# Subtracting the softmax's maximum as the bias of eight small exponentials on ScalarE, in place of one VectorE subtraction per half of the heads

## What is computed

```python
x = x + attn(cond1(x), Wq, Wk, Wv, Wo)   # cond1: per sequence a 64x64 matrix and a bias
x = x + ffn(cond2(x), w_up, w_down)      # quantised, with Walsh-Hadamard transforms
# attn, 16 heads of 32:
scores = q @ k.T / sqrt(32) + alibi_causal_bias      # 64 x 64 per sequence and head
attn   = softmax(scores, axis=-1)                    # exp(s - max) / sum
out    = (attn @ v) @ Wo.T
# ffn:
h = hbitlinear(x, w_up)       # fwht, quantise per token by its absolute maximum, matmul
h = square(relu(h))
y = hbitlinear(h, w_down)
```

## Time and profile before

| | before |
|---|---|
| median of 3 runs | 871.18 us (870.59 to 871.32) |
| profiled execution, its own time | 873.74 us |
| its span | 871.9 us |
| busy: PE, DVE, ACT, POOL | 797.4, 661.9, 376.2, 266.9 us |
| mean granted TensorE clock | 0.977 |

### The profile page before, as it was taken

The page is one execution under the profiler, slowest core; times in us unless marked ns, Lnnn a source line. Parts: engine busy times, 40 slices in busy tenths (PEclk is TensorE's granted clock), DMA queues, the critical chain, the costliest instruction groups (busy, mean ns, idle before and its releaser), DMA issues.

```text
span 871.9 us, 19069 instructions
## 1 busy us (share of the span) xinstructions
PE 797.4 (91%) x7625; PEld 681.0 (78%) x7625; DVE 661.9 (76%) x1243; ACT 376.2 (43%) x687; POOL 266.9 (31%) x324
## 2 busy tenths in 40 slices
PE   6965899999999999999999999999999999998777
PEld 4855788888888888888888888888888888786563
DVE  3455777887788778877788788877887788777864
ACT  1564245444433444444434454444334444443321
POOL 1202332333233333333233323332333333322311
PEclk8968999999999999999999999999999999999989
DMA  8521111111111101111111011111111110000000
GB/s 276 171 97 31 29 30 33 41 43 44 44 44 31 39 30 32 43 44 44 43 36 36 30 31 44 43 44 43 44 30 34 34 34 26 28 26 27 13 12 13
DMA packets 38285, 39.65 MB, mean 45 GB/s; under 512 B 21172, under 2 KB 22324, under 8 KB 38196
## 3 DMA queue, kind: packets, MB, share of 16 engines
q1 hardware_dynamic: 34436, 33.48, 12.5%
q10 hardware_dynamic: 3760, 4.95, 1.7%
HBM read 30.02 MB, written 8.39 MB: 44 GB/s over the span
## 4 chain that ended last, share of the span: by engine, by line
PE 59%; DVE 17%; POOL 10%; ACT 7%; issue 6%; ACTq 1%; DMA 1%; POOLq 0%; DVEq 0%
PE bank L322 35%; DVE hid L223 13%; POOL gT L223 9%; PE bank L499 8%; PE bank L442 7%; PE bank L412 4%; PE bank L520 3%; ACT hid L660 2%; ACT hid L658 2%; ACT gT L683 2%; PE bank L430 1%; DMA k_bd<-in_L_attn_Wk_dram 1%; ACTq L598 1%; DVE s L761 0%; DVE srow L765 0%
## 5 line engine op out<-in xcount | busy, mean ns | idle before, releaser
L223 DVE TENSOR_TENSOR hid<-hid 128x256 f32<-128x256 f32 (+1 forms) x192 | 136.1, 748 | 5.6 <-ACT hid L660 0.9
L223 POOL TENSOR_TENSOR hid<-hid 128x256 f32<-128x256 f32 x128 | 100.0, 801 | 118.4 <-DVE hid L860 115.9
L223 POOL TENSOR_TENSOR gT<-gT 128x256 f32<-128x256 f32 x124 | 87.7, 729 | 157.2 <-ACT gT L683 154.8
L499 PE MATMUL bank<-cst_sb,hid 128*128 128x128 f32 x512 | 68.5, 289 | 25.6 <-DVE hid L223 25.6
L499 PEld LDWEIGHTS bank<-cst_sb,hid 128*128 128x128 f32 x512 | 62.2, 198 | 31.8 <-DVE hid L223 31.8
L939 POOL TENSOR_TENSOR s<-s,srow 128x512 f32<-128x512 f32 x32 | 33.5, 1046 | 172.2 <-DVE srow L782 164.5
L322 PE MATMUL bank<-h_hi,wk_hi 128*128 128x256 f32 x256 | 77.4, 303 | 9.0 <-ACT v_bd L566 5.3
L678 ACT ACTIVATE late<-bank,sc 128x1024 f32<-128x1024 f32 x32 | 35.8, 1117 | 98.1 <-DVE sc L895 98.1
L918 POOL TENSOR_TENSOR h_lo<-h_sum,h_hi 128x512 fp32r<-128x512 f32 x32 | 41.0, 1285 | 113.0 <-ACT h_hi L553 105.7
L322 PE MATMUL bank<-h_hi,wq_hi 128*128 128x256 f32 x256 | 75.4, 295 | 0.0
L322 PE MATMUL bank<-h_lo,wk_hi 128*128 128x256 f32 x256 | 73.1, 286 | 0.0
(11 more groups left out here) (114 smaller groups left out, 2004.7 us busy)
## 6 DMA issues: line engine op xcount, KB each, us to landing
x_in<-in_x_dram SPq DMA_DIRECT2D x32, 256.0 KB, 2.8
x_res<-in_x_dram SPq DMA_DIRECT2D x32, 256.0 KB, 2.6
out_dram<-late SPq DMA_DIRECT2D x32, 256.0 KB, 3.1
w_bd<-in_L_cond_weights_dram SPq DMA_DIRECT2D x126, 16.0 KB, 2.0
bias_in<-in_fside_8xS_dram SPq DMA_DIRECT2D x62, 32.0 KB, 2.9
k_bd<-in_L_attn_Wk_dram ACTq DMA_DIRECT2D x1, 1024.0 KB, 5.5
s<-in_L_attn_Wq_dram ACTq DMA_DIRECT2D x1, 1024.0 KB, 8.4
v_bd<-in_L_attn_Wv_dram ACTq DMA_DIRECT2D x1, 1024.0 KB, 10.7
```

What stands on the lines that cost most here:

```text
L223: eng.tensor_tensor(dv[:, :, n], sv[:, :, 0], sv[:, :, 1], op).then_inc(done, 1)
L499: mm = pe.matmul(ps01[:, m * P:(m + 1) * P], hid[:, 1, m, :], had, start=True, stop=True)
```

## The change

The subtraction (part 2) is taken out of `softmax` on DVE, in both halves. `exp` on ACT becomes eight instructions of 128 x 64, one per head, whose bias operand is that head's entry in `srow`. So that the maximum can be used as it stands, DVE writes the negated score (the scale is negative and the ALiBi bias is subtracted), takes the minimum, and the exponential has scale -1: exp(-s' + min s') = exp(s - max s). The counts of `d_soft` fall from 14 to 12 a step. Nothing moves between DMA queues, PE and POOL.

```diff
+            def exp(p, c, half):
+
+                act.wait_ge(d_soft, p * 12 + 2 * half + 2)
+                for h in range(8 * half, 8 * half + 8):
+                    e = act.activation(s[:, c % 2, h, :], s[:, c % 2, h, :], ACT.Exp, bias=srow[:, 0, h:h + 1], scale=-1.0)
+                e.then_inc(a_exp, 1)
...
                 if attn:
-                    act.wait_ge(d_soft, p * 14 + 3)
-                    act.activation(s[:, c % 2, 0:8, :], s[:, c % 2, 0:8, :], ACT.Exp).then_inc(a_exp, 1)
+                    exp(p, c, 0)
...
                 if attn:
-                    act.wait_ge(d_soft, p * 14 + 6)
-                    act.activation(s[:, c % 2, 8:16, :], s[:, c % 2, 8:16, :], ACT.Exp).then_inc(a_exp, 1)
+                    exp(p, c, 1)
...
                     if part == 0:
                         dve.wait_ge(s_s, p * 2 + half + 1)
-                        dve.scalar_tensor_tensor(s[:, c % 2, hs, :].rearrange("p h k -> p (h k)"), bank[half], DH ** -0.5,
-                                                 alibi[:, hs, :].rearrange("p h k -> p (h k)"), ALU.mult, ALU.add).then_inc(d_soft, 1)
-                    elif part == 1:
+                        dve.scalar_tensor_tensor(s[:, c % 2, hs, :].rearrange("p h k -> p (h k)"), bank[half], -DH ** -0.5,
+                                                 alibi[:, hs, :].rearrange("p h k -> p (h k)"), ALU.mult, ALU.subtract).then_inc(d_soft, 1)
+                    else:
                         dve.wait_ge(d_soft, c0 + 1)
-                        dve.tensor_reduce(srow[:, 0, hs], s[:, c % 2, hs, :], AX.X, ALU.max).then_inc(d_soft, 1)
-                    else:
-                        dve.wait_ge(d_soft, c0 + 2)
-                        dve.tensor_tensor(s[:, c % 2, hs, :], s[:, c % 2, hs, :], srow[:, 0, hs].unsqueeze(2).broadcast_to([P, 8, T]),
-                                          ALU.subtract).then_inc(d_soft, 1)
+                        dve.tensor_reduce(srow[:, 0, hs], s[:, c % 2, hs, :], AX.X, ALU.min).then_inc(d_soft, 1)
```

More of the change, by code:

```diff
@@ L757, in softmax @@
                     hs = slice(8 * half, 8 * half + 8)
-                    c0 = p * 14 + 3 * half
+                    c0 = p * 12 + 2 * half
                     if part == 0:
                         dve.wait_ge(s_s, p * 2 + half + 1)
-                        dve.scalar_tensor_tensor(s[:, c % 2, hs, :].rearrange("p h k -> p (h k)"), bank[half], DH ** -0.5,
-                                                 alibi[:, hs, :].rearrange("p h k -> p (h k)"), ALU.mult, ALU.add).then_inc(d_soft, 1)
-                    elif part == 1:
+                        dve.scalar_tensor_tensor(s[:, c % 2, hs, :].rearrange("p h k -> p (h k)"), bank[half], -DH ** -0.5,
+                                                 alibi[:, hs, :].rearrange("p h k -> p (h k)"), ALU.mult, ALU.subtract).then_inc(d_soft, 1)
+                    else:
                         dve.wait_ge(d_soft, c0 + 1)
-                        dve.tensor_reduce(srow[:, 0, hs], s[:, c % 2, hs, :], AX.X, ALU.max).then_inc(d_soft, 1)
-                    else:
-                        dve.wait_ge(d_soft, c0 + 2)
-                        dve.tensor_tensor(s[:, c % 2, hs, :], s[:, c % 2, hs, :], srow[:, 0, hs].unsqueeze(2).broadcast_to([P, 8, T]),
-                                          ALU.subtract).then_inc(d_soft, 1)
+                        dve.tensor_reduce(srow[:, 0, hs], s[:, c % 2, hs, :], AX.X, ALU.min).then_inc(d_soft, 1)
                 def exp_sum(half):
@@ L779, in normalize @@
                     hs = slice(8 * half, 8 * half + 8)
-                    c0 = p * 14 + 6 + 4 * half
+                    c0 = p * 12 + 4 + 4 * half
                     dve.wait_ge(d_soft, c0 + 2)
@@ L802, in step @@
                 if attn:
-                    for part in range(3):
+                    for part in range(2):
                         softmax(0, part)
@@ L829, in step @@
                     dve.tensor_scalar(sc1[:, 3:4], sc1[:, 2:3], QB, D ** -0.5, ALU.mult, ALU.mult).then_inc(d_q1, 1)
-                if attn:
-                    softmax(1, 2)
                 if ffn:
@@ L937, in step @@
                     hs = slice(0, 8)
-                    pool.wait_ge(d_soft, p * 14 + 10)
+                    pool.wait_ge(d_soft, p * 12 + 8)
                     pool.tensor_tensor(s[:, c % 2, hs, :], s[:, c % 2, hs, :], srow[:, 2, hs].unsqueeze(2).broadcast_to([P, 8, T]),
```

## The result

| | before | changed |
|---|---|---|
| median | 871.25 us (870.59 to 871.84, 4 runs) | 892.83 us (891.6 to 895.99, 4 runs) |
| profiled execution, its span | 873.74, 871.9 us | 895.99, 894.0 us |

The account below looks back on a forecast made before the run. PE, nearly full, was taken as the bound, reached through ACT's string without idle time behind y1. 30 steps x 0.8 = 24.0, less 0.6 in step 0, gave +23.4: profiled 897.1, median 894.5 us, range 882 to 918.

Parts of the forecast that it names:

- The block: Eight small exponentials on ACT per half take 2.05 us in place of 0.63, at 337 ns each, overlapping.
- Rival 1: The small exponentials on ACT do not overlap; block 0.72 us longer, 1.52 a step, 916 us; chance 0.17.
- Half 0 free: Half 0's longer exponentials cost nothing, covered by ACT's wait ahead of y1; without that cover 1.42 us a step.
- The gain of 0.47: Removing half 0's 1.20 us subtraction on DVE lets L820 start only 0.47 us earlier, held by L412.
- rival 4: Small exponentials stream at a spacing below 0.11 us, q1 comes 0.47 earlier, 0.275 a step gained: 862 us; chance 0.06.
- The string: ACT's work behind half 1's exponentials, without idle time up to the first relu, runs 0.95 us later (1.42 less 0.47).
- a sign: Sign in the changed profile: PE waits about 0.6 us for ACT's copy_qk ahead of the second qk job.
- L499: PE's L499, behind DVE's butterflies, comes 0.70 to 0.95 us late, taken as 0.8 a step for steps 1 to 30.
- The ends: Outside steps 1 to 30: step 0 gains 0.6 us, step 31 changes by 0.
- Step 0's -0.6: In step 0, with no y1 in front, removing L768 saves 0.6 us in the chain of the start.
- Rival 2: Part is absorbed: the shift passed on is 0.59 us or less; 0.3 to 0.5 a step, 880 to 886; chance 0.07.
- Rival 3: New waits make TensorE's clock fall in every steady step, 28 x 1.73 = 48 us more: 943; chance 0.05.

Follow-up runs that it names:

- run 1: Kernel before with the bias form (no DVE subtraction, eight small exponentials) in half 0 alone, half 1 unchanged: 872.14 us, ratio 1.0015 to the kernel before.
- Run 2: Kernel before with the bias form in half 1 alone, half 0 unchanged: 904.68 us, ratio 1.0406 to the kernel before.
- run 8: Kernel before with 8 spare matmuls in PE's wait ahead of L499 in steps 30 and 31: 867.28 us, ratio 0.996 to the kernel before.
- run 7: Changed kernel with spare matmuls in PE's waits ahead of L458 and L499 in steps 30 and 31: 888.77 us, ratio 1.0206 to the kernel before.
- run 10: Changed kernel with PE's waits filled, spare matmuls, copy_qk ahead of half 1's exponentials and spread_k behind oT_hi: 847.57 us, ratio 0.9738 to the kernel before.
- run 11: Kernel before (softmax unchanged) with PE's waits filled, spare matmuls, and copy_qk and spread_k moved on ACT: 856.34 us, ratio 0.984 to the kernel before.
- run 12: Kernel before with PE's waits filled, spare matmuls, bias form in half 0 alone, no moves on ACT: 847.18 us, ratio 0.9745 to the kernel before.

## Why the prediction was right

- **The block.** Eight exponentials were forecast at 2.05 us and took 2.01 to 2.02; one takes 336 ns (337 forecast), and they overlap as the two L574 do. Rival 1, the spacing of the L566, did not occur. The Trainium skill's "ScalarE: Activation LUTs", section "What ACT_TABLE_LOAD costs", gives 2013 ns for eight, an estimate from its figures; by that rule, the trace agrees.
- **Half 0 free.** Its block ended at 412.71, 1.65 us ahead of `y1`; run 1 shows it.
- **The gain of 0.47.** Half 1's exponentials start 3.55 us behind L412 (414.94 - 411.39), before 4.02. DVE now waits 0.68 us ahead of L821 for L412, which is where nearly all of the other 0.73 of the 1.20 went. Run 2 shows the same 0.46 by its absence. In the kernel before, L820 waited for nothing (its row shows no idle time); the prediction's remark under rival 4, that the trace shows DVE waiting at L820, misread it.
- **The string.** Measured from L412, the copy is 0.91 later, the first relu 0.88 (forecast 0.95 both); L442 0.60 (0.59); L458 0.88 (0.87); DVE's copy L862 0.88 (0.87); the butterflies, by their row at 422.20, 0.70 (0.70). The second qk job starts 0.52 later (forecast 0.59), but only 0.26 of it shows as PE's idle time, where about 0.6 was given as a sign.
- **L499.** 0.74 late in this step, and 0.69 in the mean over 28. The forecast took 0.8 between 0.70 and 0.95; the measured 0.69 lies just below. This is the term that was mis-sized, by 0.11 a step or 3.3 us over 30: the butterflies on DVE were hardly slowed by POOL's later ones, as I had allowed for (3.82 us from their start to L499, before 3.78), so L499 moved nearly as they did.
- **The ends.** Step 0's -0.6 did not show: L412 of step 2 is 0.7 later. The first scores on PE (L384) were already 0.41 late at 36.36, ahead of anything changed, and POOL's reduction began 5.7 us behind its input in place of 4.2. The profiles cannot tell what the change did there: in run 8, whose start is that of the kernel before, L412 of step 2 stands at 102.36 in place of 105.42, so two profiles differ there by more than the change. At the other end step 30 lost more than 0.8, since the clock fell one step earlier than in the profile of before: L412 to L412 27.21 in place of 23.60, and step 31 24.18 in place of 25.68. Where spare matmuls keep the clock up (runs 7 and 8), step 30 takes 24.48 and 23.58, and step 31 22.68 and 22.77: 0.8 more for the two together, as forecast.
- **How close the number is.** Part of it is luck. Of the 23.4 us forecast between the profiles 22.1 came. The 28 steps gave 3.1 less than forecast (19.3 for 22.4), the start 0.5 more (0.7 for 0.2) and the end 1.3 more (2.1 for 0.8), for reasons that the sum did not have. Against the median the forecast is 1.7 us high, against the profiled execution 1.1 (897.1 for 895.99): the changed kernel's profiled execution is 3.16 us above its median, not 2.56.
- **Rival 2**, a shift of 0.59 or less, did not occur either, since the relu's way was the longer one. **Rival 3**, the clock in the steady steps, did not occur: 1.00 from 100 to 800 us. **Rival 4** needed a spacing of 0.11 us and had 0.24. But the mechanism in it, DVE's `q1` coming just in time for PE, is real: runs 10 to 12 show it once PE arrives a third of a microsecond earlier. Its price came out near (0.275 a step; 856.34 - 847.57 = 8.8 us, 24.35 - 24.04 = 0.31 a step), by luck: the 0.275 was a wait of the weight loads that cost PE nothing in the kernel before, and it is 0.52 a step in run 11 (8.3 over 16). The condition was incomplete too: it was tied to the exponentials' length and not to when PE arrives.

## What to carry to other kernels

An engine that is busy 43% of the time can be full in just the stretch that counts: follow the string of its instructions without idle time up to the next wait of another engine, and price an added operation by whether it stands inside. Work taken off an engine pays up to the next thing that it waits for, here 0.47 of 1.88 us, and half 0's subtraction, whose removal was worth nothing against the kernel before, was worth 1% when TensorE's waits were filled. When a longer operation reaches the bound by two ways, cutting one shows little; try both together before dropping the idea.

## What was unexpected of the hardware

- Four ACTIVATEs of 64x256 out of PSUM (L566) take 1.54 us at 377 ns each and do not overlap, while eight of 128x64 in SBUF at 336 ns take 2.01 and overlap by 0.10 each. What makes the difference is open; no run varied it.
- TensorE's granted clock falls to its lower level near the end, in the two profiles at different places: in that of the kernel before around the 2.01 us in which PE stood ahead of L499 of step 31 (0.85 in the mean over 833 to 835 us, 0.50 over 835 to 837), and in that of the changed kernel during L458 of step 30, behind 1.94 us of standing (1.00 over 826 to 827.3, 0.69 over 827.3 to 829, 0.50 over 829 to 836.2). L499 takes 3.78 us at the lower level and 2.05 at the upper one.
